# Unused places of a scatter tile: from skipped by a bounds check to written into spare rows

## The chip, the cores and the metric

One core of one Trainium2 chip runs the whole program. The metric is the device time of one execution in microseconds (us), lower is better. The kernel before took 1118.82 us (median of three runs, 1118.78 to 1120.42).

## What is computed

One transformer layer in float32 on x of 4 x 512 tokens with 512 features:

```
x = x + layernorm(attention(layernorm(x)))          # 16 heads, rotary positions, causal
xt = layernorm(x)                                   # 2048 tokens
top_w, top_i = top_k(softmax(xt @ router_w.T), 8)   # 8 of 64 experts, weights made to sum to 1
routed = sum over a token's 8 experts e of
         w[token, e] * (silu(xt @ Wg[e].T) * (xt @ Wu[e].T)) @ Wd[e].T      # F = 128
shared = sigmoid(xt @ Wse.T) * ((silu(xt @ Wsg.T) * (xt @ Wsu.T)) @ Wsd.T)
out = x + layernorm(routed + shared)
```

The 2048 x 8 = 16384 pairs of token and expert are what the change is about.

## The kernel before, in words

Five engines run their own instruction streams and wait for each other on semaphores: TensorE (PE, with its weight loads PEld), VectorE (DVE), ScalarE (ACT), GpSimd (POOL) and the DMA queue of SyncE (SP).

**Stages.** Attention runs to about 400 us. Then come the output projection, the router and, from about 480 us, the shared expert; beside it the kernel builds a table that sorts the 16384 pairs by expert into tiles of 128 places. Each expert begins a new tile, so the last tile of an expert has unused places. `token_i` holds, by partition and tile, the number of the token of that place, or NOWHERE. NOWHERE is 3 x 2048 = 6144, one past the last row of the sum tables.

**Expert loop** (about 560 to 1062 us, 157 tiles: 26 bodies of 6 tiles and one more). Each tile passes these steps:
- POOL, line 469 (`gather`): an indirect DMA fetches the 128 tokens' rows (512 features and 64 weights, 2304 bytes) from `x2_rows` into one of six row buffers. Seven tiles are gathered ahead with `first_i`; an unused place gathers row 2047.
- PE, line 1036: four transposes of the rows; ACT, line 703, takes them out of PSUM.
- PE, line 1043: eight matmuls with the expert's gate and up weights; ACT, line 708, the silu; DVE, line 1428, the product times the weight of the pair.
- PE, line 1049: a transpose; DVE, line 1442, takes it out. PE, line 1054: the down projection.
- DVE, line 1437 (`take_y`): makes the scatter's index; line 1438 takes the result out of PSUM into one of six buffers `y_sb`.
- POOL, line 474 (`scatter`): an indirect DMA that adds the tile's 128 rows of 2048 bytes to a table of sums in DRAM (`sum_rows`).

There are three sum tables of 2048 rows. Tile t goes to table (t + 1) mod 3, as two adding transfers in flight must not meet in a row. So POOL, before the scatter of tile t, waits until that of tile t - 3 has landed (`pass_tile`), and DVE, before it fills a `y_sb` buffer, until that of tile t - 6 has landed. POOL's order is fixed by hand, per tile: the gather of a later tile, when its row buffer has been read (line 1036, and line 1422 for the weight) and its index is staged (line 1413), then the scatter of this one. SP reloads the ring of eight expert weight buffers (768 KB each) in the same stretch.

**The scatter before.** The index of a place is the token's number plus 2048 times the table's number. The instruction carries a bound, the last row of the tables, held in a register, and a place above it is left out without an error. An unused place (6144 and more) is always above it.

**After the loop** POOL waits for all scatters and releases SP (`s_routed`), which reads the three tables back (line 398). PE and DVE add them, and the last layer norm and the output follow.

Of the kernel before, what the change touches and what calls it, by code (L numbers as in the profile page):

```python
# [7 lines left out]
FP32 = mybir.dt.float32  # L8
# [3 lines left out]
ALU = mybir.AluOpType  # L12
AX = mybir.AxisListType

P = 128
B, S, D = 4, 512, 512
# [21 lines left out]
TABLES = 3  # L38
# [19 lines left out]
FIRST_STEPS = [("xt", 0), ("xt", 1), ("proj", 0), ("xt", 2), ("proj", 1), ("xt", 3), ("proj", 2), ("qkt", 0),  # L58
               ("proj", 3), ("qkt", 1)]

NOWHERE = TABLES * B * S
SUM_ON_PE = tuple(i for i in range(TILES) if i not in (0, 3, 5, 8, 10, 13, 15))

NORM_X_AT = (BLOCKS - 6, BLOCKS - 5, BLOCKS - 3, BLOCKS - 2)
# [2 lines left out]
def sandwich_kernel(nc, x, wqkv, wo, router, experts, rope, mask, ident, before, ones, upto, below,  # L67
                    steps, count, token, out):
    ctx = ExitStack()
    with ctx:  # L70
        def sb(name, shape, dtype=FP32):
            return ctx.enter_context(nc.sbuf_tensor(name, shape, dtype))

        def sem(name):
            return ctx.enter_context(nc.semaphore(name))
# [17 lines left out]
        token_sb = sb("token_sb", [P, TILES])  # L93
# [4 lines left out]
        small = sb("small", [P, 4, 8])  # L98
# [12 lines left out]
        token_i = sb("token_i", [P, COLS], INT32)  # L111
        idx = sb("idx", [P, DEEP, 2], INT32)
# [58 lines left out]
        def table_of(q):  # L171
            return (q + 1) % TABLES
# [7 lines left out]


        x2_rows = nc.dram_tensor("x2_rows", (B * S, XROW), FP32).ap()
        all_sums = nc.dram_tensor("sum_rows", (TABLES * B * S, D), FP32).ap()
        sum_rows = [all_sums[p * B * S:(p + 1) * B * S, :] for p in range(TABLES)]
        all_sums_v = all_sums.rearrange("(s t p) d -> p t s d", s=TABLES, p=P)

        ps = ctx.enter_context(nc.psum_tensor("ps", [P, 8, 512], FP32))
        s_bank = [ps[:, i, :] for i in range(HG)]
# [117 lines left out]
        s_scatter = [sem(f"s_scatter{p}") for p in range(TABLES)]  # L306
# [98 lines left out]
        def _(pool):  # L405
# [66 lines left out]
            def scatter(q):  # L472
                p = table_of(q)
                pool.indirect_dma_start(all_sums, bass.IndirectOffsetOnAxis(ap=idx[:, q, 1:2], axis=0), y_sb[q],  # L474
                                        None, bounds_check=last_sum, oob_is_err=False,
                                        compute_op=ALU.add).then_inc(s_scatter[p], 16)

            last_sum = pool.to_reg(TABLES * B * S - 1)
            for p in range(2):
                pool.wait_ge(s_x2d[p], 16 * (TILES // 2))  # L480
            pool.wait_ge(s_combd, 16)
# [10 lines left out]
            def pass_tile(j, c, gathers):  # L492
                t = j * DEEP + (c + 1)
                if gathers:
                    pool.wait_ge(s_idx, t)
                    pool.wait_ge(s_xg_ps, t + 1)
                    pool.wait_ge(s_weight, t + 1)
                    pool.sem_inc(s_issue, 1)
                    gather((c + 1) % DEEP, idx[:, (c + 1) % DEEP, 0:1])
                pool.wait_ge(s_y, t)  # L500
                pool.wait_ge(s_scatter[table_of(c)], (j * 2 + (c // TABLES + 2)) * 16)
                pool.sem_inc(s_issue, 1)
                scatter(c)
# [7 lines left out]
            pool.wait_ge(s_scatter[table_of(0)], (full * 2 + 4) * 16)  # L511
            pool.sem_inc(s_issue, 1)
            scatter(0)
            for q in range(DEEP):
                pool.wait_ge(s_gather[q], (full + (2 if q < 3 else 1)) * 16)
# [587 lines left out]
        def _(dve):  # L1103
# [117 lines left out]
            def step(ins):  # L1221

                own[0] += 1
                ins.then_inc(s_own, 1)
                dve.wait_ge(s_own, own[0])
# [158 lines left out]
            def tokens(lo, hi):  # L1384

                step(dve.tensor_copy(stepped_f[:, lo:hi + 1], ps[:, 7, lo:hi + 1]))
                step(dve.tensor_tensor(out=step_d[:, lo:hi], in0=stepped_f[:, lo + 1:hi + 1], in1=stepped_f[:, lo:hi],
                                       op=ALU.subtract))
                step(dve.scalar_tensor_tensor(out=table_f[:, lo:hi], in0=step_d[:, lo:hi], scalar=0.5, in1=ps[:, 6, lo:hi],
                                              op0=ALU.mult, op1=ALU.add))  # L1390
                step(dve.tensor_scalar(table_z[:, lo:hi], table_f[:, lo:hi], 0.0, float(NOWHERE + 1), ALU.is_equal, ALU.mult))
                return dve.scalar_tensor_tensor(out=token_i[:, lo:hi], in0=table_f[:, lo:hi], scalar=-1.0,
                                                in1=table_z[:, lo:hi], op0=ALU.add, op1=ALU.add)
# [4 lines left out]
            step(tokens(HEAD, HIGH))  # L1398
            dve.memset(token_i[:, HIGH:COLS], NOWHERE).then_inc(s_table, 1)


            wcol = small[:, 0, 0:2]

            def shared_late(i):

                dve.wait_ge(s_silu, i + 1)
                bank = ps[:, 7 if i == TILES - 1 else 2 + i % 2, 0:GATEUP]
                dve.tensor_tensor(out=late_hidden[:, i - EARLY, :], in0=late_gate[:, i - EARLY, :], in1=bank[:, F:GATEUP],
                                  op=ALU.mult).then_inc(s_late, 1)
# [21 lines left out]
            def take_y(t, q, r):  # L1431

                dve.wait_ge(s_dn, t + 2)
                dve.wait_ge(s_scatter[table_of(q)], r)
                if q == 2:
                    dve.wait_ge(s_ysh, 48)
                dve.tensor_scalar(idx[:, q, 1:2], token_i[:, bass.ts(t, 1)], table_of(q) * B * S, None, ALU.add)
                dve.tensor_scalar(y_sb[q], ps[:, 5 + q % 2, :], 1.0, None, ALU.mult).then_inc(s_y, 1)  # L1438

            def take_hidden(t, p):  # L1440
# [16 lines left out]
            with dve.Fori(0, quads) as j:  # L1457
                for c in range(DEEP):
                    t = j * DEEP + (c + 1)
                    hide(t, (c + 1) % 2)  # L1460
                    take_y(t - 1, c, (j * 2 + (c // TABLES + 1)) * 16)
                    take_hidden(t, (c + 1) % 2)
                    q = (c + 2) % DEEP
                    weight(t + 1, q, (j + (1 + (c + 2) // DEEP)) * 16)
                    stage_gather(t + (DEEP + 1), q)
            take_y(quads * DEEP, 0, (quads * 2 + 1) * 16)


# [83 lines left out]
```

## Time and profile before

| | |
|---|---|
| median of three runs | 1118.82 us (1118.78 to 1120.42) |
| profiled execution, its own time | 1119.89 us |
| its span in the trace | 1118.1 us |
| PE / DVE / ACT / POOL busy | 94% / 60% / 45% / 53% of the span |
| granted TensorE clock, mean | 0.988 of full speed |
| DMA moved | 179.95 MB, mean 161 GB/s |

Busy time counts what an engine executes. DMA instructions on POOL are shown with the time in which POOL prepares the transfer (its busy time); from issue to landing, which takes longer, is given apart. In the list of instruction groups a row has the line, engine, operation, output<-input, count, then total busy us and mean ns of one, then the idle time before them and what ended it. "issue" is time in which the engine waited for nothing that the profile shows. In a timeline a row has start and length in us, engine, line, operation, and in brackets the idle time before it and what ended it; times count from the span's start.

### The profile page before, as it was taken

The page shows a single profiled execution, that of the slowest core. Times are in us where ns is not written, and L with a number is a line of the kernel's source. Part 1 is how long each engine was busy: PE and PEld are TensorE (multiplying, and loading weights), DVE is VectorE, ACT ScalarE, POOL GpSimd, SP SyncE. Part 2 cuts the span into 40 slices and gives each one's busy share as a digit, 9 for nine tenths or more (in the row PEclk, how much of TensorE's full clock was granted, in tenths as well). Part 3 has the DMA queues.
Part 4 walks back from the last instruction along what each step waited for, and adds up shares of the span by engine and source line. Part 5 has one row for each costly group of instructions (what it writes and reads, how often), then busy time and mean ns, then how long its engine had stood idle before and what let it go on. Part 6 is the DMA issues. An engine that isn't in the chain of part 4 may idle for free.

```text
span 1118.1 us, 23361 instructions
## 1 busy us (share of the span) xinstructions
PE 1055.4 (94%) x6269; PEld 718.6 (64%) x6270; DVE 665.5 (60%) x2336; ACT 501.3 (45%) x1422; POOL 590.3 (53%) x616
## 2 busy tenths in 40 slices
PE   5999999999999979999999999999999999999954
PEld 3565666666666545556667777777777677777721
DVE  5666666666666668879745554445445454455548
ACT  2766676666676654447632222222222222222224
POOL 3643433433434403310257788878888787878710
PEclk9999999999999999989999999999999999999988
DMA  9830000000000043112289999999999999998888
GB/s 331 312 143 1 1 2 1 2 1 1 1 2 1 2 161 123 57 38 77 88 243 230 243 246 275 243 267 253 285 254 282 250 247 295 282 254 173 156 299 316
DMA packets 68368, 179.95 MB, mean 161 GB/s; under 512 B 13456, under 2 KB 15248, under 8 KB 68176
## 3 DMA queue, kind: packets, MB, share of 16 engines
q0 software_dynamic: 38496, 93.08, 35.3%
q1 hardware_dynamic: 29808, 86.07, 21.7%
q8 instruction: 34, 0.56, 0.2%
q14 instruction: 30, 0.25, 0.1%
HBM read 119.85 MB, written 66.85 MB: 167 GB/s over the span
## 4 chain that ended last, share of the span: by engine, by line
PE 72%; DMA 15%; DVE 6%; issue 3%; ACT 2%; POOL 2%; SPq 0%; POOLq 0%; DVEq 0%; ACTq 0%
PE ps L1043 16%; PE ps L761 15%; DMA sum_rows<-x_t,idx 12%; PE ps L1054 8%; PE ps L820 7%; PE ps L879 5%; PE ps L790 4%; PE ps L1036 4%; PE ps L840 4%; PE ps L912 2%; PE ps L775 2%; DMA x_t<-x_rows,idx 2%; PE ps L895 1%; PE ps L1049 1%; POOL x_t L469 1%
## 5 line engine op out<-in xcount | busy, mean ns | idle before, releaser
L1043 PE MATMUL ps<-big,work 128*128 x1264 | 299.3, 380 | 0.0
L474 POOL DMA_INDIRECT sum_rows<-x_t,idx x157 | 250.2, 1593 | 56.8 <-issue 32.8
L1043 PEld LDWEIGHTS ps<-big,work 128*128 128x128 f32 x1264 | 228.3, 191 | 24.3
L761 PE MATMUL ps<-big 128*128 128x384 f32 x512 | 178.6, 493 | 2.1 <-ACT big L536 1.7
L469 POOL DMA_INDIRECT x_t<-x_rows,idx x152 | 150.0, 987 | 51.4 <-issue 26.7
L703 ACT ACTIVATE work<-ps 128x512 f32<-128x512 f32 x159 | 94.9, 597 | 170.1 <-PE ps L1036 165.2
L416 POOL TENSOR_TENSOR work<-qkv_all,rope_sb 128x256 f32<-128x256 f32 x64 | 46.6, 728 | 222.6 <-ACT qkv_all L541 222.6
L1054 PE MATMUL ps<-big,work 128*128 x314 | 160.5, 593 | 0.1
L1036 PEld LDWEIGHTS ps<-ident_sb,x_t 128*128 128x128 f32 x636 | 77.5, 141 | 94.5 <-issue 77.9
L560 ACT ACTIVATE work<-ps,neg_max 128x128 f32<-128x128 f32 (+3 forms) x256 | 131.9, 529 | 0.3
L708 ACT ACTIVATE work<-ps 128x128 f32<-128x128 f32 x158 | 43.8, 277 | 196.0 <-PE ps L1043 196.0
L1164 DVE CUSTOM_DVE_ANT_0 ps<-ps,mask_sb 128x128 f32<-128x128 f32 (+3 forms) x256 | 120.4, 512 | 15.8 <-PE ps L790 13.9
L761 PEld LDWEIGHTS ps<-big 128*128 128x128 f32 x512 | 93.3, 192 | 56.2 <-ACT big L536 3.4
L1428 DVE SCALAR_TENSOR_TENSOR work<-work,small,ps 128x128 f32<-128x128 f32 x157 | 54.5, 347 | 124.2 <-ACT work L708 123.9
L566 ACT ACTIVATE x_t<-ps 128x128 f32<-128x128 f32 (+2 forms) x192 | 77.0, 436 | 82.6 <-PE ps L820 82.6
L1438 DVE TENSOR_SCALAR x_t<-ps 128x512 f32<-128x512 f32 x157 | 106.8, 681 | 0.0
L1036 PE MATMUL ps<-ident_sb,x_t 128*128 128x128 f32 x636 | 96.5, 274 | 6.2 <-DMA x_t<-x_rows,idx 4.4
L820 PE MATMUL ps<-ident_sb,work 128*128 128x128 f32 x640 | 97.4, 283 | 0.8 <-ACT x_t L566 0.8
L820 PEld LDWEIGHTS ps<-ident_sb,work 128*128 128x128 f32 x640 | 68.3, 141 | 36.7 <-issue 30.7
L1185 DVE TENSOR_TENSOR attn_t<-ps,work 128x128 f32<-128x128 f32 x64 | 18.6, 291 | 107.0 <-PE ps L840 107.0
L1422 DVE TENSOR_SCALAR small<-x_t 128x1 f32 x158 | 24.3, 154 | 70.3 <-issue 68.7
L1054 PEld LDWEIGHTS ps<-big,work 128*128 128x128 f32 x314 | 59.7, 190 | 8.8 <-issue 0.9
(185 smaller groups left out, 1433.3 us busy)
## 6 DMA issues: line engine op xcount, KB each, us to landing
big<-experts SPq DMA_DIRECT2D x65, 768.0 KB, 7.1
sum_rows<-x_t POOLq DMA_DIRECT2D x6, 2048.0 KB, 20.4
big<-sum_rows SPq DMA_DIRECT2D x8, 768.0 KB, 9.6
x_rows<-work SPq DMA_DIRECT2D x16, 256.0 KB, 2.0
out<-x_sb SPq DMA_DIRECT2D x16, 256.0 KB, 5.4
x_sb<-x SPq DMA_DIRECT2D x3, 1024.0 KB, 10.5
x_t<-sum_rows SPq DMA_DIRECT2D x4, 768.0 KB, 13.2
attn_t<-sum_rows SPq DMA_DIRECT2D x4, 768.0 KB, 13.4
```

The source lines that it names most:

```text
L469: pool.indirect_dma_start(rows[q], None, x2_rows, bass.IndirectOffsetOnAxis(ap=at, axis=0)).then_inc(s_gather[q], 16)
L474: pool.indirect_dma_start(all_sums, bass.IndirectOffsetOnAxis(ap=idx[:, q, 1:2], axis=0), y_sb[q], None, bounds_check=last_sum, oob_is_err ...
L560: act.activation(probs[:, h, 0:n], s_bank[h][:, 0:n], ACT.Exp, bias=neg_max[:, h:h + 1], scale=-1.0, accum_out=den[:, h:h + 1]).then_inc(s ...
L566: act.activation(probs_t[:, i % 2, h, 0:qt + 1, :], pt_bank[h % 2].rearrange("p (k n) -> p k n", k=TB)[:, 0:qt + 1, :], ACT.Copy).then_inc ...
L703: act.activation(rows_t[:, p, :, :], ps[:, p, :].rearrange("p (c n) -> p c n", c=DC), ACT.Copy).then_inc(s_xg, 1)
L761: mm = pe.matmul(bank[:, 0:QKV], x_t[:, c, bass.ts(t, P)], wqkv_sb[:, c, g % G, :], start=(c == 0), stop=(c == DC - 1))
L820: mm = pe.transpose(pt_bank[h % 2][:, bass.ts(c, P)], probs[:, h, bass.ts(c, P)], ident_sb[:, :])
L1036: mm = pe.transpose(ps[:, p, bass.ts(c, P)], rows[q][:, bass.ts(c, P)], ident_sb[:, :])
L1043: mm = pe.matmul(ps[:, 2 + p, 0:GATEUP], rows_t[:, p, c, :], w_ring[:, slot, c * GATEUP:(c + 1) * GATEUP], start=(c == 0), stop=(c == DC - 1))
L1054: pe.matmul(ps[:, 5 + p, :], hidden_t[:, p, :], w_ring[:, slot, DC * GATEUP:WCOLS], start=True, stop=True).then_inc(s_dn, 1)
L1164: dve.tensor_tensor_reduce(sc, sc, mask_sb[:, S - n:S], -SCALE, 3.0e38, ALU.add, ALU.min, neg_max[:, h:h + 1]).then_inc(s_masked, 1)
L1438: dve.tensor_scalar(y_sb[q], ps[:, 5 + q % 2, :], 1.0, None, ALU.mult).then_inc(s_y, 1)
```

## The change

- The sum table tensor grows by 3 x 128 rows behind the three tables, and NOWHERE becomes 3 x (2048 + 128) = 6528. The read-back still covers the three tables alone.
- The scatter loses its bounds check and the register with the bound.
- DVE, once ahead of the expert loop, makes three columns `unused_row`: for partition p and table s the row 6144 + 128 s + p.
- The index instruction (line 1437 before) becomes the smaller of token + 2048 s and `unused_row`, so an unused place adds its row to its own spare row. Places that hold a token keep their index.

```diff
-NOWHERE = TABLES * B * S
+NOWHERE = TABLES * (B * S + P)
...
-        all_sums = nc.dram_tensor("sum_rows", (TABLES * B * S, D), FP32).ap()
+        all_sums = nc.dram_tensor("sum_rows", (TABLES * (B * S + P), D), FP32).ap()
         sum_rows = [all_sums[p * B * S:(p + 1) * B * S, :] for p in range(TABLES)]
-        all_sums_v = all_sums.rearrange("(s t p) d -> p t s d", s=TABLES, p=P)
+        all_sums_v = all_sums[0:TABLES * B * S, :].rearrange("(s t p) d -> p t s d", s=TABLES, p=P)
...
                 pool.indirect_dma_start(all_sums, bass.IndirectOffsetOnAxis(ap=idx[:, q, 1:2], axis=0), y_sb[q],
-                                        None, bounds_check=last_sum, oob_is_err=False,
-                                        compute_op=ALU.add).then_inc(s_scatter[p], 16)
-
-            last_sum = pool.to_reg(TABLES * B * S - 1)
+                                        None, compute_op=ALU.add).then_inc(s_scatter[p], 16)
+
...
             wcol = small[:, 0, 0:2]
+            unused_row = small[:, 1, 0:TABLES]
+            for p in range(TABLES):
+                step(dve.tensor_scalar(unused_row[:, p:p + 1], token_sb[:, 0:1], float(TABLES * B * S + p * P - 1), None, ALU.add))
...
-                dve.tensor_scalar(idx[:, q, 1:2], token_i[:, bass.ts(t, 1)], table_of(q) * B * S, None, ALU.add)
+                dve.tensor_scalar(idx[:, q, 1:2], token_i[:, bass.ts(t, 1)], float(table_of(q) * B * S), unused_row[:, table_of(q):table_of(q) + 1],
+                                  ALU.add, ALU.min)
```

`step` issues a DVE instruction and makes DVE wait for its end.

## Rows read from the trace of the kernel before

**Rows 1.** The page's list of instruction groups, the two indirect DMAs.
```profile
L474 POOL DMA_INDIRECT sum_rows<-x_t,idx x157 | 250.2, 1593 | 56.8 <-issue 32.8
...
L469 POOL DMA_INDIRECT x_t<-x_rows,idx x152 | 150.0, 987 | 51.4 <-issue 26.7
```

**Rows 2.** The timeline of POOL from 602 to 608 us, early in the expert loop.
```profile
602.64 0.99 POOL L469 DMA_INDIRECT x_t<-x_rows,idx  x1 [0.30 <-DMA sum_rows<-x_t,idx]
603.93 1.59 POOL L474 DMA_INDIRECT sum_rows<-x_t,idx  x1 [0.30 <-issue]
605.83 0.99 POOL L469 DMA_INDIRECT x_t<-x_rows,idx  x1 [0.30 <-issue]
```

**Rows 3.** The timeline of PE, the down projections of two successive tiles.
```profile
602.97 1.02 PE L1054 MATMUL ps<-big,work 128*128 x2
...
606.10 1.02 PE L1054 MATMUL ps<-big,work 128*128 x2
```

**Rows 4.** Lines 1054 and 474 by themselves: duration in ns min/median/max, first and last start.
```profile
L1054 PE MATMUL ps<-big,work x314: 592/592/692, 562.8 to 1062.4; 128*128 x157
...
L474 POOL DMA_INDIRECT sum_rows<-x_t,idx x157: 1552/1594/1629, 565.8 to 1064.8; - x157
...
DMA to landing us min/median/max: 3.1/7.0/10.2
```

**Rows 5.** The timeline: index and scatter of tiles 6 and 96 (counted from 0).
```profile
585.07 0.15 DVE L1437 TENSOR_SCALAR idx<-token_i 128x1 int32 x1 [0.42 <-PE ps L1054]
...
587.51 1.60 POOL L474 DMA_INDIRECT sum_rows<-x_t,idx  x1 [0.30 <-issue]
...
869.82 0.15 DVE L1437 TENSOR_SCALAR idx<-token_i 128x1 int32 x1 [0.42 <-PE ps L1054]
...
876.52 1.60 POOL L474 DMA_INDIRECT sum_rows<-x_t,idx  x1 [0.30 <-DMA sum_rows<-x_t,idx]
```

**Rows 6.** The timeline of PE: tile 7, a body's boundary, and a wait for a gather.
```profile
587.30 1.02 PE L1054 MATMUL ps<-big,work 128*128 x2
...
697.01 1.02 PE L1054 MATMUL ps<-big,work 128*128 x2
...
700.40 1.02 PE L1054 MATMUL ps<-big,work 128*128 x2
...
884.26 1.02 PE L1054 MATMUL ps<-big,work 128*128 x2
...
887.13 0.66 PE L1036 MATMUL ps<-ident_sb,x_t 128*128 128x128 f32 x4 [1.85 <-DMA x_t<-x_rows,idx]
...
889.46 1.02 PE L1054 MATMUL ps<-big,work 128*128 x2
```

**Rows 7.** Line 440 by itself: POOL's six direct DMAs of 1024 rows of 2048 bytes.
```profile
L440 POOL DMA_DIRECT2D sum_rows<-x_t x6: 885/890/1106, 30.7 to 35.4; - x6
```

**Rows 8.** The chain that ended last: start, us, from a scatter's start to its landing.
```profile
1009.23 4.98 DMA sum_rows<-x_t,idx
...
1064.83 3.06 DMA sum_rows<-x_t,idx
```

**Rows 9.** DMA from 600 to 1000 us: queues (share of 16 engines), then issues.
```profile
q0 software_dynamic: 28014, 63.76, 69.8%
q1 hardware_dynamic: 7496, 40.93, 29.4%
...
sum_rows<-x_t,idx POOLq DMA_INDIRECT x125, 7.2
```

**Rows 10.** The same view from 1012 to 1050 us, when no expert is loaded any more.
```profile
q0 software_dynamic: 2689, 6.06, 84.1%
...
sum_rows<-x_t,idx POOLq DMA_INDIRECT x12, 5.1
```

**Rows 11.** The timeline of DVE ahead of the loop, where the three new instructions go.
```profile
547.76 0.16 DVE L1389 SCALAR_TENSOR_TENSOR qkv_all<-qkv_all,ps 128x8 f32<-128x8 f32 x1
...
551.38 0.29 DVE L1408 TENSOR_TENSOR work<-work,ps 128x128 f32<-128x128 f32 x1 [0.83 <-ACT work L656]
```

## The prediction

> **What bounds the kernel now.** The page's list of instruction groups comes first. The scatter, which the change touches, costs POOL 1593 ns and the gather 987 ns [rows 1]. The timeline of POOL shows what they make of the pace: 0.30 + 0.99 + 0.30 + 1.60 = 3.19 us per tile (602.64 to 605.83), with nothing but the fixed 0.30 us ahead of each [rows 2]. PE, at full clock, needs 3.13 us per tile (602.97 to 606.10) [rows 3]. So two engines are nearly tied, and POOL is the slower by 0.06 us. Over the loop POOL wins: line 1054 starts its first tile at 562.8 us and line 474 its last at 1064.8 us [rows 4]; from tile 7 (587.30) to the last down projection (its second half starts at 1062.4, so the pair at 1061.9) there are 149 steps in 474.6 us, 3.185 us each, where PE alone would take 149 x 3.133 = 466.8 us [rows 3, 4, 6]. (3.133 is the mean over undisturbed tiles; the two rows shown differ by 3.13.) PE loses 7.8 us.
>
> Why PE loses them is read from the distance between a tile's index on DVE and its scatter on POOL. It is 2.4 us at tile 6 and 6.7 us at tile 96 [rows 5]: POOL falls behind by 4.3 us in 90 tiles, nearly 90 x 0.057 = 5.1 us. The gathers stand in the same queue, so they come late too, until a row buffer isn't filled when PE wants it: the transpose at 887.13 waits for its gather, and the step from 884.26 to 889.46 lasts 5.20 us, 2.07 over the pace [rows 6]. Such a stop gives POOL some microseconds back, and it begins again; there are three such stretches (near 790, 887 and 930 us).
>
> Not all 7.8 us are POOL's. Eight steps, most of them at the boundary between two bodies of six tiles, are 0.1 to 0.35 us over the pace, as 697.01 to 700.40 with 3.39 us [rows 6]; I sum them to 1.8 us and leave them in. POOL's share is 7.8 - 1.8 = 6.0 us.
>
> **The scatter without a bounds check.** The trace of before has no adding indirect DMA without a check, so I bound it. From below stands the gather with 987 ns [rows 1]: also 128 indices, no check, no add. From above stands the scatter's own 1593 ns, if the check costs nothing; I know no reason for more. Nearest is the gather, as the operation is the same but for the add. What the add may cost POOL is one more read entry for each of 128 rows. A direct DMA of 1024 rows takes POOL 885 ns [rows 7], under 0.9 ns per row, so 128 more entries would be some 0.1 us; I allow 0.2 us, as an indirect DMA makes them one by one. I take 1.2 us, 0.4 us less than now, and keep 0.99 and 1.59 for the range.
>
> POOL's cycle becomes 0.30 + 0.99 + 0.30 + 1.20 = 2.79 us, under PE's 3.13. POOL can no longer fall behind; anything under 1.53 us does as well. The gain in the loop is then 6.0 us however short the scatter gets, and PE is late next. Gathers come as early as at tile 6, before the lag grew.
>
> A rule of the Trainium skill speaks against this. Its page "Collectives: The Full Stack" (The bandwidth ceiling: the fold count and why AG ≠ RS ≠ AR) says that an adding transfer carries two read descriptors per chunk where a copy has one. If POOL's time went by read descriptors, 987 ns doubled would more than fill 1593 ns with nothing left for the check; by that the sum would be 1121.8 us. The row of the direct DMA, with its 1024 rows in 885 ns, speaks against counting so, and no row shows the adding form by itself.
>
> **The unused places.** 157 tiles have 20096 places for 16384 pairs, so 3712 are unused, 23.6 per tile. They move nothing now: from 600 to 1000 us 125 gathers and 125 full scatters would be 36.9 + 32.8 = 69.6 MB, and the queue moved 63.76 MB [rows 9]. They will move 3712 x 2 KB = 7.6 MB. In DMA engine time (mean over 16), q0 takes 69.8% of 400 us for 63.76 MB, 4.4 us per MB, and in the quiet stretch 84.1% of 38 us for 6.06 MB, 5.3 us per MB [rows 9, 10]. So 33 to 40 us are added; if all of the quiet stretch's time were its 12 scatters' (3.1 MB) it would be 10 us per MB and 77 us. Over a loop of 490 us the share goes up by 0.07 to 0.08, at most 0.16. The sum of both queues is 0.99 now. It is no full pipe: q0 alone had 84.1% without experts and has 69.8% beside their 29.4%, at the same pace of tiles [rows 9, 10], so packet times contain waiting and shrink. What load does is lengthen landings: the experts' 0.294 raised the scatter's median from 5.1 to 7.2 us [rows 9, 10], 0.7 us per 0.1. For 0.08 this gives +0.6 us (at most +1.1), less 0.4 us of shorter preparation: about 7.4 us. A scatter has 3 x 3.13 = 9.4 us before the one three tiles later needs it landed. The longest landing, 10.2 us [rows 4], may become 11; that holds POOL up by 1.6 us, which it makes good in five tiles at 0.34 us each, while its gathers have several us to spare. DVE's wait for the scatter six tiles back has 18.8 us. Cost in the loop: nothing; without that cover, each late landing would go into the sum.
>
> **The tail.** The last tile is nearly empty and its scatter lands in 3.06 us, where a full one in the quiet stretch takes 4.98 us [rows 8]. SP's read-back waits for it, so 1.9 us are added on the path, less the 0.4 us of preparation: +1.5 us (0 if an empty tile's length hardly mattered, +1.9 if preparation stays).
>
> **DVE.** Three instructions of one column, each like the 0.16 us at 547.76, some 0.6 us with their waits, go ahead of line 1408. DVE idles 0.83 us before the second of these (551.38) [rows 11], so they cost nothing; uncovered they would cost 0.6 us. The index of line 1437, 0.15 us [rows 5], gets a second operation and a pointer; I leave it at that. DVE's time in the loop is hidden under PE, and a rise to 0.16 us would be too. The register on POOL is one instruction outside the loop.
>
> **Sum.** Profiled execution 1119.9 - 6.0 + 1.5 = 1115.4 us. That execution is 1.1 us above the median of 1118.8; before's runs spread over 1.6 us, about what one waiting stretch more or less costs, and without those stretches I expect no such offset. Against the median the gain is 3.4 us, 0.3%. A measurement of this kernel can tell about 0.2%, 2.2 us, from no change.
>
> **Rivals.**
> First, slower: the check costs POOL nothing. Place: line 474; it decides as soon as the scatter without the check takes over 1.53 us. POOL's cycle stays 3.19 us, nothing is gained, the tail adds 1.9 us, and landings 0.6 us longer now hold a POOL that cannot catch up, 0 to 3 us: 1121.8 to 1125. For it: the add may cost the 606 ns between the two indirect forms. Against: 1024 rows in 885 ns [rows 7], and 0.06 us are enough. 14%.
> Second, slower too: landings take over. If they pass 9.4 us as a rule, the three tables set the pace, a third of the landing per tile; 9.8 us would be 3.27 us per tile, 156 x 0.13 = 21 us more, about 1137 us. For it: a summed share of 0.99 [rows 9]. Against: the shrinking packet times and 2 us between the median and 9.4. 7%. The Trainium skill's page "DMA: Bandwidth & Descriptors" (Latency and other measured facts) gives HBM's latency as 0.2 us on average and 2 us at high load, which would be 9.0 us here, still short of it.
> Third, about the same: POOL's cycle shrinks as I say, but PE's stops come from bursts on the DMA engines and half of them stay. 1119.9 - 3.0 + 1.5 = 1118.4. Against: the lag rises steadily before each stop. 10%.
>
> **How the numbers follow.** The forecast has 69%. Its own range is 1113.5 (boundary stops gone too) to 1117.5 (a stop left, preparation 1.53 us). Of it 58 points are faster by over 0.2% and 11 within. The first rival gives 11 slower and 3 the same, the second 6 slower and 1 the same, the third 2 faster and 8 the same; rounding gives 0.60, 0.23, 0.17. The range goes from 1113.0 to 1122.5, into the first rival, and leaves out its upper part, the second and a little below.
>
> **What would show it.** Right: line 474 well under 1.53 us per scatter; a constant distance from index to scatter of about 2 us; no idle time of line 1036 behind a gather; 3.13 us per tile; median landing 7 to 8 us; the last scatter landing in about 4.6 us. q0 moves 100.7 MB. Wrong: 1.6 us at line 474 and a lag that still grows, or POOL idle before line 474 behind the landing of an earlier scatter.

## The result, and the profile after

The change made the kernel slower: 1125.39 us (median of five runs, 1123.81 to 1127.95) against 1118.78 us for the kernel before (five runs, 1115.69 to 1120.42), a ratio of 1.0062 [1.0042, 1.0083], 0.6%. I had forecast 1115.4 us in a range to 1122.5, with 0.17 on slower. What happened is the first rival: the scatter's time on POOL didn't change, so nothing was gained, and the tail grew. How much the rows cost in the loop is less certain, as the experiments will show.

The page's list of instruction groups and its DMA queue, kernel after (line 1438 is line 1437 of before, 1052 is 1054, 1034 is 1036; POOL's two lines keep their numbers):

```profile
q0 software_dynamic: 38496, 100.65, 37.4%
...
L474 POOL DMA_INDIRECT sum_rows<-x_t,idx x157 | 250.2, 1593 | 62.7 <-issue 40.4
L469 POOL DMA_INDIRECT x_t<-x_rows,idx x152 | 150.0, 987 | 51.0 <-issue 25.1
...
L1438 DVE TENSOR_SCALAR idx<-token_i,small 128x1 int32 x157 | 33.6, 214 | 54.7 <-PE ps L1052 46.8
```

The first indirect row settles the main term: 250.2 us and 1593 ns, digit for digit what stands in [rows 1]. Without its check the scatter takes POOL exactly as long. q0 moved the 100.65 MB that I had expected. The last row is a surprise of no weight: the index takes 214 ns instead of some 150.

The DMA view from 600 to 1000 us, kernel after:

```profile
q0 software_dynamic: 27355, 68.05, 72.8%
q1 hardware_dynamic: 7439, 40.69, 29.7%
...
sum_rows<-x_t,idx POOLq DMA_INDIRECT x123, 7.3
x_t<-x_rows,idx POOLq DMA_INDIRECT x122, 7.0
```

And the gathers from 600 to 1000 us in the kernel before:

```profile
x_t<-x_rows,idx POOLq DMA_INDIRECT x125, 6.5
```

From 1012 to 1050 us, kernel after:

```profile
q0 software_dynamic: 2834, 7.04, 93.5%
...
sum_rows<-x_t,idx POOLq DMA_INDIRECT x13, 5.1
```

Beside [rows 9, 10], q0's share rose by 3 points with experts and by 9 without, and the scatter's median landing by 0.1 us and by nothing. The gather's median rose more, from 6.5 to 7.0 us with experts. The loss itself shows in PE's waits. The view of waits from 560 to 1070 us, kernel after, and behind it the same of before (engine, line, what it waited for: us in total, times, longest):

```profile
PEld ps L1034 <- DMA x_t<-x_rows,idx: 25.5, 31, 2.2
...
PE ps L1034 <- DMA x_t<-x_rows,idx: 8.4, 11, 1.7
```

```profile
PEld ps L1036 <- DMA x_t<-x_rows,idx: 14.2, 24, 2.7
```

(The whole view of before has 4.4 us in 4 places for PE itself at line 1036.) The transposes waited for gathered rows almost twice as long. One of these places, the timeline of POOL and then of PE, kernel after:

```profile
782.78 0.99 POOL L469 DMA_INDIRECT x_t<-x_rows,idx  x1 [0.30 <-issue]
...
789.16 0.99 POOL L469 DMA_INDIRECT x_t<-x_rows,idx  x1 [0.30 <-issue]
791.56 1.59 POOL L474 DMA_INDIRECT sum_rows<-x_t,idx  x1 [1.42 <-DVE idx L1414]
793.46 0.99 POOL L469 DMA_INDIRECT x_t<-x_rows,idx  x1 [0.30 <-DMA sum_rows<-x_t,idx]
```

```profile
786.49 1.02 PE L1052 MATMUL ps<-big,work 128*128 x2
788.50 0.66 PE L1034 MATMUL ps<-ident_sb,x_t 128*128 128x128 f32 x4 [0.99 <-DMA x_t<-x_rows,idx]
790.84 1.02 PE L1052 MATMUL ps<-big,work 128*128 x2
792.60 0.66 PE L1034 MATMUL ps<-ident_sb,x_t 128*128 128x128 f32 x4 [0.74 <-DMA x_t<-x_rows,idx]
794.93 1.02 PE L1052 MATMUL ps<-big,work 128*128 x2
```

And the chain of waits there:

```profile
782.78 9.78 DMA x_t<-x_rows,idx
792.55 0.04 issue
792.60 0.66 PE ps L1034 x4
```

The gather issued at 782.78 lands 9.78 us later, at 792.56, and PE turns at 792.60: the two steps from 786.49 to 794.93 last 8.44 us where 6.27 would do. PE had wanted these rows at 791.86, where its idle time begins, 9.1 us after the issue. In the same stretch POOL stood idle for 1.42 us ahead of the scatter at 791.56. The row names DVE's line 1414, but that is the index of a gather and had long been done. What the scatter does wait for is its own index and result, ready some 7 us before, and the landing of the scatter three tiles back (780.88), which would have taken 10.4 us. The trace gives no landing for that one; the next scatter, issued at 784.07, took 9.6 us. So I read it as a landing, by exclusion.

**Where the 8.0 us of the two profiled spans lie** (1126.1 less 1118.1, each stretch read from the timelines):

| stretch | before | after | difference |
|---|---|---|---|
| start to the first down projection | 562.8 | 562.3 | -0.5 |
| from there to tile 7 | 24.5 | 23.8 | -0.8 |
| tile 7 to the last, over 149 x 3.133 us | 7.8 | 14.0 | +6.2 |
| last down projection to the read-back | 6.2 | 8.3 | +2.1 |
| read-back to the end | 50.0 | 51.0 | +1.0 |

In the loop, 11 of after's steps exceed the pace by over 0.5 us (10.8 us in all), against 4 of before (5.3 us). POOL's idle time ahead of scatters beyond the fixed 0.30 us is 9.5 us in 19 places against 3.3 in 9 (tile 10 to four tiles from the end; 10.4 and 3.8 us up to the last tile but one, where an expectation below has 9.9). These are two single executions.

The tail, in the chain that ended last, kernel after, as [rows 8] for before:

```profile
1069.81 5.09 DMA sum_rows<-x_t,idx
...
1075.14 0.39 SPq L398
```

The full last scatter lands in 5.09 us, where the nearly empty one took 3.06.

### The profile page after: what moved, and what is told of

Same layout as the page of the kernel before. It is cut to its first block, busy times and chain, and to the rows that moved or that the text cites. A ratio compares the mean times of both kernels' runs of the same rounds, so it can differ in the third digit from the quotient of the medians.

```text
span 1126.1 us, 23364 instructions
## 1 busy us (share of the span) xinstructions
PE 1057.2 (94%) x6269; PEld 717.0 (64%) x6270; DVE 675.9 (60%) x2339; ACT 501.7 (45%) x1422; POOL 590.3 (52%) x616
## 2 busy tenths in 40 slices
DMA packets 68368, 187.53 MB, mean 167 GB/s; under 512 B 9744, under 2 KB 11536, under 8 KB 68176
## 3 DMA queue, kind: packets, MB, share of 16 engines
q0 software_dynamic: 38496, 100.65, 37.4%
## 4 chain that ended last, share of the span: by engine, by line
PE 68%; DMA 17%; DVE 6%; issue 3%; POOL 2%; ACT 2%; SPq 0%; POOLq 0%; DVEq 0%; ACTq 0%
PE ps L759 15%; PE ps L1041 14%; DMA sum_rows<-x_t,idx 11%; PE ps L818 7%; PE ps L1052 7%; DMA x_t<-x_rows,idx 5%; PE ps L877 5%; PE ps L788 4%; PE ps L838 4%; PE ps L1034 4%; PE ps L773 2%; PE ps L910 2%; POOL x_t L469 1%; PE ps L893 1%; POOL sum_rows L474 1%
## 5 line engine op out<-in xcount | busy, mean ns | idle before, releaser
L474 POOL DMA_INDIRECT sum_rows<-x_t,idx x157 | 250.2, 1593 | 62.7 <-issue 40.4
L1041 PEld LDWEIGHTS ps<-big,work 128*128 128x128 f32 x1264 | 227.9, 190 | 24.5
L1034 PE MATMUL ps<-ident_sb,x_t 128*128 128x128 f32 x636 | 96.9, 275 | 10.4 <-DMA x_t<-x_rows,idx 8.4
L1438 DVE TENSOR_SCALAR idx<-token_i,small 128x1 int32 x157 | 33.6, 214 | 54.7 <-PE ps L1052 46.8
```

The costliest lines, as they stand in the source:

```text
L1034: mm = pe.transpose(ps[:, p, bass.ts(c, P)], rows[q][:, bass.ts(c, P)], ident_sb[:, :])
L1041: mm = pe.matmul(ps[:, 2 + p, 0:GATEUP], rows_t[:, p, c, :], w_ring[:, slot, c * GATEUP:(c + 1) * GATEUP], start=(c == 0), stop=(c == DC - 1))
```

## The experiments

The times below are medians, each beside the kernel before on the same chip: 1119.83 us (29 runs) for the four whose names begin with e, 1119.5 (20) for those with i, r and c, 1118.76 (14) for the two with h. "Loop loss" is the time from tile 7 to the last down projection over 149 x 3.133 us, read from each profile. Part 1 asks what the add and the check cost POOL, part 2 what the rows cost and where, part 3 why.

### Part 1: what do the 606 ns belong to?

**e1_plain_write**, against the kernel after. The scatter writes its rows instead of adding them, so the sums over experts are left out.

```diff
-                                        None, compute_op=ALU.add).then_inc(s_scatter[p], 16)
+                                        None).then_inc(s_scatter[p], 16)
```

> The kernel after, whose scatter writes its rows instead of adding them (the sums are left out; indices, rows and waits stay). Theory A (the add, not the check, is what a scatter costs POOL over a gather): line 474 falls from 1593 to about 990 ns, POOL's cycle to 2.6 us, under PE's 3.133; PE's stops behind gathers vanish and the 149 tile steps take 467 to 469 us (after: 480.8, before: 474.6), so 10 to 14 us less than after, about 1112 to 1115. Theory B (1593 ns are fixed for a scatter by its 2048-byte rows or its direction): line 474 stays near 1.59 us and the loop near 475 us or more. Both expect less load on the DMA engines, as no row is read before it is written.

Measured: 1125.57 us, ratio 1.0051 [1.0027, 1.0075]. The page's groups:

```profile
q0 software_dynamic: 28448, 100.65, 25.2%
...
L474 POOL DMA_INDIRECT sum_rows<-x_t,idx x157 | 155.0, 987 | 149.0 <-issue 65.4
```

The plain scatter, also without a check, costs POOL 987 ns, just what the gather of [rows 1] costs: the 606 ns are the add's. The same bytes also count 10048 packets fewer, 64 for each of 157 scatters.

The total missed what a POOL with slack should give. POOL's lag was gone (some 3 us from down projection to scatter, but for the stops), the queue's share had fallen by a third, and still PE lost 11.4 us in the loop, 10.4 of them in seven steps over the pace by more than 0.5 us. The view of waits has no gather among what PE waited for. The timeline of the longest:

```profile
674.45 0.60 PE L1034 MATMUL ps<-ident_sb,x_t 128*128 128x128 f32 x4
...
677.17 0.28 ACT L706 ACTIVATE work<-ps 128x128 f32<-128x128 f32 x1 [4.62 <-remote]
677.48 0.35 DVE L1429 SCALAR_TENSOR_TENSOR work<-work,small,ps 128x128 f32<-128x128 f32 x1 [4.28 <-ACT work L706]
...
677.88 0.47 PE L1047 MATMUL ps<-ident_sb,work 128*128 128x128 f32 x1 [2.84 <-DVE work L1429]
```

ACT begins the silu after 4.62 us of idle time, released by something that the profile can't name ("remote"), and PE follows. By the program it waits there for PE's line 1041, whose row ends 3.4 us earlier, at 673.75. What held it I didn't find out. Behind the stop the granted clock is 0.55 from 678 to 681 us, and the eight matmuls of line 1041 take 3.19 us instead of 1.89. Five of the seven steps, 9.1 of the 10.4 us, have such a "remote" row in them; the loops of the other kernels have none. So this variant's total says nothing of what the add costs the kernel; its row on POOL does.

**e3_check_passes_all**, against the kernel after. The check comes back with a bound at the last spare row, so that it lets every place through.

```diff
+                                        None, bounds_check=last_sum, oob_is_err=False,
+                                        compute_op=ALU.add).then_inc(s_scatter[p], 16)
...
+            last_sum = pool.to_reg(TABLES * (B * S + P) - 1)
```

> The kernel after with a bounds check at the last spare row, which every index passes. Theory A (the check is free and the rows cost): line 474 at 1593 ns and the time of after, 1125.4 within 2 us. Theory B (the check costs POOL something that the traces of before and after hide): line 474 longer than 1.6 us and over 1127 us.

Measured: 1126.64 us, 1.0067 [1.0041, 1.0094], the same as the kernel after (1.0062). Its group on the page:

```profile
L474 POOL DMA_INDIRECT sum_rows<-x_t,idx x157 | 250.2, 1594 | 61.0 <-issue 45.2
```

With or without a check, 1593 or 1594 ns. The check is free, in the time of POOL and in the total.

### Part 2: what do the spare rows cost, and where?

**e2_index_only**. As e3, but the bound is the last row of the tables again (`TABLES * B * S - 1`): unused places are left out, while the new index and its three columns on DVE stay.

> The kernel after with the bounds check put back at the last row of the tables: the new index on DVE and the larger tensor stay, unused places are skipped as before. Theory A (what costs is the rows that unused places now move): as before, 1118.8 within 2 us, POOL waits before line 474 of some 4 us in the loop, median step loss as before, 6 to 8 us; the index takes 214 ns instead of 154 and is hidden. Theory B (the 60 ns longer index, or what DVE does to POOL, holds the loop up): as after, 1124 to 1127.

Measured: 1122.07 us, 1.0015 [0.9997, 1.0033], 2.2 us over the kernel before and so just outside the 2 us of Theory A. From e3 it differs in the bound's value alone, and in 3712 rows written: 4.6 us by the medians, and the two intervals don't meet. Part of that may be the clock's: all four runs of e3 have a mean granted clock of 0.987, and the three of e2 with 0.987 average 1123.2 us against e3's 1127.0, which leaves 3.8. In the profiles the loop lost 11.1 us here and 11.4 in e3, and PE and PEld waited 6.8 and 20.3 us for gathers here, 5.1 and 19.2 in e3. So the rows' cost in the loop doesn't show in this pair of single executions; the tail does, with 6.5 us from the last down projection to the read-back against 9.1.

**i_index_longer**, against the kernel before: two more index instructions of one column per tile on DVE.

```diff
+                for k in range(2):
+                    dve.tensor_scalar(spare_i[:, 2 * q + k:2 * q + k + 1], token_i[:, bass.ts(t, 1)], table_of(q) * B * S, None, ALU.add)
```

> The kernel before with two further instructions of 128x1 in front of each index instruction on DVE (written to spare columns), some 0.3 us per tile, five times what the change added to the index. Theory A (the index is hidden under PE and POOL's lag): as before, within 1.5 us. Theory B (the longer index is part of the loss): 3 us or more over before.

Measured: 1119.67 us, 0.9998 [0.9984, 1.0013]. Index time on DVE is hidden, as the prediction had it. So the 2.2 us of e2 over the kernel before aren't explained by the index's length; its interval takes in no change at all, and I leave them open. The profiled loop lost 6.7 us here.

**e4_last_tile_only**. The kernel before's index for all tiles but the last, whose unused places go to spare rows; the check is back.

```diff
-            take_y(quads * DEEP, 0, (quads * 2 + 1) * 16)
+            take_y(quads * DEEP, 0, (quads * 2 + 1) * 16, spare=True)
```

> Unused places are skipped as before (bound at the last spare row, indices above it), but for the last tile, number 156, whose 127 unused places write to their spare rows. Theory A (part of the loss is the tail: the last scatter lands later): the last scatter lands about 5 us after its start instead of 3.1, everything ahead as before, so 1120.5 to 1121. Theory B (the last scatter is hidden, or lands as fast): 1118.8 within 1 us.

Measured: 1122.17 us, 1.0017 [1.0002, 1.0032]. The chain that ended last shows the tail, this variant and then e2, where the last tile is nearly empty:

```profile
1067.39 4.81 DMA sum_rows<-x_t,idx
...
1072.44 0.39 SPq L398
```

```profile
1068.81 3.35 DMA sum_rows<-x_t,idx
```

The landing grows by 1.5 us on the path. In the medians the two differ by 0.1 us, less than either interval can tell, so the tail's size rests on the profiles: +2.1 us in the pair before and after, +1.5 here, +2.5 between e2 and e3. The profiled loop lost 10.3 us, though it writes no spare row before its last tile. So full-load loops without the rows lost 6.7 (i_index_longer), 7.8 (before), 10.3 (this one) and 11.1 us (e2), and those with them 11.4 (e3) and 14.0 (after): the spread without rows is 4.4 us, most of the 6.2 us between before and after.

### Part 3: is it POOL's lack of slack, the sum of loads, or the rows by themselves?

**r_before_direct** and **r_after_direct**: the two kernels with the indirect gather replaced by a plain transfer of the same size from the first 128 rows. Gathering is left out: all tiles compute on the same tokens. The bytes stay, the time of POOL per tile falls under PE's.

```diff
-                pool.indirect_dma_start(rows[q], None, x2_rows,
-                                        bass.IndirectOffsetOnAxis(ap=at, axis=0)).then_inc(s_gather[q], 16)
+                pool.dma_start(rows[q], x2_rows[0:P, :]).then_inc(s_gather[q], 16)
```

> The kernel before with each indirect gather replaced by a direct DMA of the table's first 128 rows, issued by POOL at the same place with the same waits (the gathering is left out, all else and the bytes stay). It frees POOL while the scatters still add and skip unused places. Theory A (POOL's 3.19 us cycle is what costs PE its 6 us): POOL's cycle falls under 3.1, the lag of scatter behind down projection stays at some 3 us, PE loses 1 to 3 us over its 149 steps instead of 7.8, about 1114. Theory B (stops come from late DMA landings whatever POOL does, as PE lost 11 us in the plain-write kernel with a free POOL): PE still loses 6 us or more, 1118 or above.

Measured: 1110.66 us, 0.9921 [0.9894, 0.9947], 3 us under Theory A's forecast. The loop loses 1.0 us instead of 7.8, no step is over the pace by 0.5 us, and the distance from down projection to scatter is 2.8 us at the median from tile 24 on, at most 3.8, instead of growing to 8. What POOL waits for in the loop is now work, not landings. Line 473 is the scatter:

```profile
L473 POOL DMA_INDIRECT sum_rows<-x_t,idx x157: 1532/1595/1664, 560.6 to 1052.6; - x157
...
  DVE x_t L1437: 88.2, 84
...
  DMA sum_rows<-x_t,idx: 3.0, 3
```

A POOL with slack is worth what the prediction said, 6 to 7 us in the loop, as far as one profile of each tells. Two things go with it. The gather has another form here, and the trace gives no landings for it, so earlier issue and faster landing aren't told apart. And the profiled run also reaches its first down projection 5.2 us earlier than that of before (557.6 against 562.8), which has nothing to do with POOL in the loop; the last section comes back to it.

> The kernel after with the same replacement of the gathers. Theory A (the rows of unused places hurt only because a POOL without slack cannot make good a late landing): PE loses as little as in the kernel before with that replacement, within 2 us, and only the tail's 2 us remain between them. Theory B (the added rows lengthen the loop by themselves): PE loses 4 us or more than there.

Measured: 1114.42 us, 0.9933 [0.9914, 0.9953]. The loop loses 2.6 us, again without a stop, and the read-back starts 8.0 us after the last down projection against 5.9. From r_before_direct to this the loop's loss grows by 1.6 us and the tail by 2.1. The medians differ by 3.8 us (1114.42 less 1110.66), but that they agree with the 3.7 is partly luck: the two profiled spans differ by 7.7 us, 4.6 of it ahead of the first down projection.

The 1.6 us aren't waits for rows. All of them lie in the 24 steps at a boundary between two bodies of six tiles, which lose 1.0 us in r_before_direct and 2.6 here. One of them takes 3.58 us (PE, this variant):

```profile
753.37 1.02 PE L1051 MATMUL ps<-big,work 128*128 x2
754.63 0.65 PE L1033 MATMUL ps<-ident_sb,x_t 128*128 128x128 f32 x4 [0.24 <-issue]
...
756.95 1.02 PE L1051 MATMUL ps<-big,work 128*128 x2
```

Whether the spare rows have a part in these boundary steps no run tells. In the profiles of before, after, e2, e3, e4 and i they sum to between 0.3 and 1.8 us without stops of over 0.5 us, and to 1.6 in before and after alike.

**h_before_quarter** and **h_after_quarter**: the two kernels, but SP reloads only the first quarter of each expert's weights in the loop, so three quarters stay another expert's. POOL keeps its cycle of 3.19 us; only the load beside it goes.

```diff
-                    sp.dma_start(w_ring[:, r, :], experts[j * NW + (r + NW)]).then_inc(s_wl[r], 16)
+                    sp.dma_start(w_ring[:, r, 0:WCOLS // 4], experts[j * NW + (r + NW)][:, 0:WCOLS // 4]).then_inc(s_wl[r], 16)
```

> The kernel before, but SyncE reloads only the first quarter of each expert's weights in the loop (192 KB instead of 768 KB); the other three quarters stay those of an earlier expert, so part of the loading is left out. POOL's cycle stays 3.19 us per tile against TensorE's 3.133. Theory A (a POOL without slack loses what late landings of scatters cost, and landings are late because the expert loads and the rows share the DMA engines): the scatter's median landing falls from 7.2 to about 5.5 us, POOL's idle time ahead of scatters from 3.8 us to under 1, but the lag of 0.057 us per tile is still there, so TensorE still loses 5 to 7 us over 149 tiles: 1117 to 1119. Theory B (POOL's waits are not from landings): idle time stays near 3.8 us and the time unchanged within 1 us.

> The changed kernel with the same relief: only the first quarter of each expert's weights is reloaded in the loop. Theory A: the landings are short again, POOL's idle time ahead of scatters falls from 9.9 us to under 2, the loop's loss from 14.0 us to 6 to 8 (what remains is the lag of a POOL 0.06 us per tile too slow), and of the difference to the kernel before only the tail's 2 us is left: 2 us above h_before_quarter, 1119 to 1121. Theory B (the 3712 spare rows cost the loop by themselves, not through the sum with the loads): the loss stays 11 us or more and the difference to h_before_quarter 5 to 6 us.

Measured: 1114.02 us, 0.9969 [0.9955, 0.9983], and 1118.73 us, 0.999 [0.9972, 1.0007]. The DMA view from 600 to 1000 us, kernel before and then kernel after with a quarter of the loads:

```profile
q0 software_dynamic: 28106, 64.09, 80.6%
q1 hardware_dynamic: 7632, 10.42, 8.7%
...
x_t<-x_rows,idx POOLq DMA_INDIRECT x126, 4.7
sum_rows<-x_t,idx POOLq DMA_INDIRECT x125, 5.2
```

```profile
q0 software_dynamic: 28013, 69.68, 87.2%
q1 hardware_dynamic: 7496, 10.24, 9.5%
...
x_t<-x_rows,idx POOLq DMA_INDIRECT x126, 4.9
sum_rows<-x_t,idx POOLq DMA_INDIRECT x126, 5.4
```

The landings and waits are those of Theory A: landings fall by 2 us and POOL's idle time ahead of scatters by all of its 3.3 us before and from 9.5 to 0.3 after, though the scatter still takes 1594 ns. PE's own waits for gathers fall from 4.4 us to 1.1 before and from 8.4 to none after. The loop loses 3.6 and 5.6 us. Of the 6.2 us between the loops with full loads 2.0 are left, and these lie at the boundaries between bodies again (1.8 us lost there before, 5.5 after); the rest of the loop loses 1.8 us before and nothing after. The tail differs by 1.0. The totals missed both forecasts: 1114.0 where I had 1117 to 1119, and 1118.7 where I had 1119 to 1121. The loss of the kernel before was 3.6 where I had written 5 to 7; the lag grows to 9.5 us at tile 144 with only 1.5 us lost in stops, and I read that as gathers issued late that still arrive. And the medians' 4.7 us lie above the 2 that Theory A named: the profiles have 2.0 of them in the loop, and the runs of h_after_quarter have the lower mean clock (0.9878 against 0.9892). In the profiled runs the first down projection comes 5.5 us later in h_after_quarter (563.2 against 557.7).

**c_pairs**, against the kernel before. POOL's order is two gathers, then two scatters. The question was whether POOL pays for each switch between the two kinds.

```diff
-                for c in range(DEEP):
-                    pass_tile(j, c, True)
+                for c0 in range(0, DEEP, 2):
+                    for c in range(c0, c0 + 2):
+                        pass_gather(j, c, True)
+                    for c in range(c0, c0 + 2):
+                        pass_scatter(j, c)
```

> The kernel before, with POOL's order changed from gather, scatter, gather, scatter to two gathers, then two scatters. In the trace of before a gather after a gather takes 0.95 us and a scatter after a scatter 1.55, against 0.99 and 1.59 where they alternate. Theory A (the switch costs 0.04 us each): 0.08 us less per two tiles, cycle 3.15 instead of 3.19; over 150 tiles POOL falls behind PE by 2.5 us instead of 8, and PE loses 3 to 5 us less: 1115 to 1117 against 1119. Theory B (the longer preparation comes from other traffic): 0.99 and 1.59 stay, and the time is as before or 1 us over it, since scatters come later.

Measured: 1137.74 us, 1.0148 [1.0115, 1.0181], far over both forecasts. The timeline of POOL over one pair:

```profile
650.02 1.02 POOL L469 DMA_INDIRECT x_t<-x_rows,idx  x1 [0.30 <-DVE x_t L1446]
651.34 0.99 POOL L469 DMA_INDIRECT x_t<-x_rows,idx  x1 [0.30 <-issue]
652.63 1.62 POOL L474 DMA_INDIRECT sum_rows<-x_t,idx  x1 [0.30 <-issue]
654.56 1.58 POOL L474 DMA_INDIRECT sum_rows<-x_t,idx  x1 [0.30 <-issue]
656.44 1.01 POOL L469 DMA_INDIRECT x_t<-x_rows,idx  x1 [0.30 <-DMA sum_rows<-x_t,idx]
```

Two tiles take 6.42 us, where alternating takes 6.38: a switch costs nothing. What the order did cost is timing. Scatters are issued later (mostly 7 to 11 us behind the down projection), and I read the rest as two of them close together meeting the landing three tiles back: POOL's idle time ahead of scatters rises from 3.3 us in 9 places to 19.0 in 23, and the loop loses 26.2 us. It is the strongest sign of how thin this loop's cover is, though lateness and waits aren't told apart by it.

No variant that computes the whole layer was faster than the kernel before. A way to shorten POOL's cycle without changing what is gathered would be the one to look for.

## Why the prediction was wrong, point by point

**What bounds the kernel: right.** POOL's cycle of 3.19 us against PE's 3.13, the growing lag, and late gathers as the form of the loss stood up to every run. With POOL under PE's pace (r_before_direct) the loop's loss went from 7.8 to 1.0 us; I had priced POOL's share at 6.0. (The steps that are 0.1 to 0.35 us over the pace are nine and sum to 2.1 us, not eight and 1.8, which makes that share 5.7.)

**The scatter without a bounds check: the step that failed.** I took 1.2 us between 0.99 and 1.593, and it is 1.593, the upper end. The 606 ns belong to the add (e1_plain_write) and none of them to the check (e3_check_passes_all, the change itself). The error was in the argument for the near end: I priced the add's entries by a direct DMA of 1024 rows in 885 ns [rows 7], and took the count of rows as the measure of POOL's work. An indirect transfer of 128 rows costs 987 ns and its adding form 1593, so rows of a direct transfer say nothing of either. I had two unknowns, check and add, and one difference of 606 ns; no row of the profile divided it, and I divided it by a row of another kind of instruction.

The page "Collectives: The Full Stack" of the Trainium skill (The bandwidth ceiling: the fold count and why AG ≠ RS ≠ AR) gives an adding transfer two read descriptors per chunk. These runs agree in direction: the add has a price of its own, in POOL's time and in packets. In size they don't: twice 987 ns would be 1974, and the add brings 64 packets per scatter, not 128. By that rule I had the rival's 1121.8 us, nearer than my forecast.

With 1.593 us the gain of 6.0 us is zero: that alone moves the sum from 1115.4 to 1121.4.

**The unused places, "cost in the loop: nothing": failed, as a consequence.** I wrote that a late landing would be made good at 0.34 us a tile, and that without this cover each one would go into the sum. The cover was the shorter scatter, and it never existed. Between the two full profiles the loop's loss differs by 6.2 us. But single executions differ: the profiled run of after stands 2.6 us above its median, that of before 1.1, so 1.5 us of the 8.0 are chance; and e2 and e4, which skip the unused places in the loop, lost 11.1 and 10.3 us in their profiled loops. By the medians the rows cost 4.6 us (e3 less e2), 3.8 at the same clock, of which 2.5 are the tail in the two profiles. So with full loads some 1 to 2 us are left for the loop by this estimate. That late landings are the way they cost is argued from the stops of the kernel after (11 against 4) and from the h pair, where the stops go with the load; e3 against e2 doesn't show it, and what the r and h pairs lose to the rows in the loop lies at the body boundaries.

I also overlooked the second path. I asked how long a scatter may take before the next of its table waits (9.4 us), and granted gathers "several us to spare". At a lag of 7 us a gather has some 9.1 us from issue to use (782.78 to 791.86 above), and before's longest already took 9.3. Load reaches PE through the gather's own landing as well.

**The sizes of traffic and landings: right, the share in part by luck.** 100.65 MB, as forecast. The share of the DMA engines was to rise by 0.07 to 0.08 over the loop, at most 0.16: it rose by 0.09 in the quiet stretch, but beside the experts by 0.03 only (q0 and q1 together from 99.2% to 102.5%). The scatter's median landing was 7.3 us (7.4 forecast); but the 7.4 had 0.4 us taken off for a shorter preparation that didn't come, so by its own terms the forecast was 7.8. Of the gather's landing, 0.5 us longer at the median, it says nothing.

**The tail: right.** +1.9 us for a full scatter with an unchanged preparation was the upper end; measured +2.1, 1.5 and 2.5 in three pairs, and 2.1 and 1.0 in the r and h pairs. What I left out is the 1.0 us after the read-back starts. PE idles longer ahead of it, and from 1080 us on it runs at a lower granted clock: the view of windows shows 0.76 from 1080 to 1095 us where before has 1.00. So a part of this may be the clock's.

**DVE: right.** 214 ns instead of 150 is hidden (i_index_longer).

**Rivals and chances.** The first rival named line 474, the threshold of 1.53 us and a POOL that cannot catch up, and priced it at 1121.8 to 1125; measured 1125.4. Its landings were priced at 0 to 3 us from a change in the scatter's median, which then hardly moved. Nor are the longest landings that the traces give much longer: 10.2 us before and 9.7 after for scatters (only 52 of 157 known after), 9.3 and 9.8 for gathers. It got 14%, on the strength of one row that didn't bear on it, and my range was cut through its middle. With one difference and two possible owners, it should have had about half. The second rival (landings as the pace) didn't come: the median stayed at 7.3. The third, stops from bursts on the DMA engines, was set against my first step, and is half right on the other side: load on the DMA engines does cost, when POOL has no slack (7.8 us lost in the loop, 3.6 in h_before_quarter).

## What to carry to other kernels

When one unexplained difference has two possible owners, no distant row divides it: look for a row of the same kind of instruction that differs in one of them, and give both owners a chance that moves the forecast. And where two engines are tied within 2% and chained by transfers, a median landing that stands still doesn't make extra bytes free: look at the stops and at every transfer on the path, and compare several executions before a difference of a few us is put down to one of them. A bounds check that skips unused places costs this kernel nothing and saves their traffic.

## What the runs showed of the hardware that I had not expected

- **The add is what an adding indirect scatter pays for on POOL:** 1593 ns for 128 rows of 2048 bytes, 987 ns for the same scatter writing, 1593 to 1594 ns with or without a bounds check, whether places are skipped or not. A skipped place still leaves a packet under 512 bytes: the page counts 13456 of them in before and 9744 in after, 3712 fewer, the number of unused places.
- **A direct transfer of 128 rows prepared by POOL isn't cheaper by its own time** (1165 ns at line 469 of r_before_direct, against 987 ns indirect), yet POOL's cycle falls under PE's with it: in the timeline its span begins before that of the scatter ahead of it has ended (at 702.01, where the scatter runs from 700.61 to 702.20), which no indirect one does.
- **The clock explains much of the spread from run to run.** Of the kernel before's 63 runs beside the experiments, the 17 with a granted mean clock of 0.991 average 1118.1 us and the 20 at 0.987 or less 1121.7. One place of it is in the traces. The view of windows from 488 to 496 us (us; busy time of PE, PEld, DVE, ACT, POOL; granted clock; DMA share; GB/s), kernel before, then h_before_quarter, whose code is the same there:

```profile
488.00:496.00 8.00, 8.00 (x25) 5.70 (x24) 3.66 (x21) 4.67 (x8) 1.09 (x3) 0.60 0.01 4
```

```profile
488.00:496.00 8.00, 7.57 (x29) 4.01 (x27) 6.37 (x36) 4.31 (x9) 0.46 (x1) 1.00 0.01 2
```

In the first PE was granted its lower level, 1.2 GHz, for most of 8 us, and eight matmuls of line 912 took 3.72 us instead of 1.95. The loop then begins at 562.8 us in the one and at 557.7 in the other. Ahead of the drop PE had had pauses (it waited 0.41 and 1.07 us for ACT ahead of its transposes), but so it had, 1.06 us, in the run that kept its clock. Such a dip, of half or all of this length, is in the profiles of all seven kernels with the change's new columns (0.83 or 0.91 from 480 to 500 us) and in that of before, and in none of the four variants of before. The five runs of after have a mean clock of 0.9862, before's 63 one of 0.9888, and before's runs change by 0.76 us per 0.001; by that some 2 of the 6.6 us would go with the clock, as an estimate. The new columns are written near 550 us, after the dip. Whether the change has a part in the clock, or its longer stops, or chance, no run here tells.
- **Waits released by something unnamed ("remote")** of up to 4.6 us on ACT and DVE, seven of them in five steps, appeared when the scatter wrote instead of added (e1_plain_write), and those steps lost 9.1 us. Their cause stays open.
